# Gate columns in the experts' product, the choice of the expert behind it, and the mixing four groups of steps later

## The reference

```python
p0, p1 = E0[tokens] @ W0 + b0, E1[tokens] @ W1 + b1        # 75 -> 64
alpha = softmax over the two of (p @ Wa + ba);  h = alpha0*p0 + alpha1*p1
x = layernorm(h)
scores = (x @ Q[h].T) @ (x @ K[h].T).T / sqrt(64)          # 8 heads of 32
h = h + sum over heads of softmax(scores) @ x @ VO[h]
x = layernorm(h)
H = gelu(x @ W1 + b1)                                      # 64 -> 256
probs = softmax(H @ Wg + bg);  e = argmax(probs)           # 8 experts
h = h + probs[e] * (H @ Wd[e] + bd[e])
```

## Time and profile before

| | us |
|---|---|
| median of 3 runs | 494.83 |
| lowest, highest | 492.53, 495.33 |
| profiled execution, its own time | 487.88 |
| its span, first to last instruction | 486.0 |
| busy: TensorE, VectorE, ScalarE, GpSimd | 453.8, 330.1, 234.2, 194.1 |

### The profile page before, as it was taken

The page is one execution under the profiler, slowest core; times in us unless marked ns, Lnnn a source line. Parts: engine busy times, 40 slices in busy tenths (PEclk is TensorE's granted clock), DMA queues, the critical chain, the costliest instruction groups (busy, mean ns, idle before and its releaser), DMA issues.

```text
span 486.0 us, 7338 instructions
## 1 busy us (share of the span) xinstructions
PE 453.8 (93%) x2026; PEld 261.1 (54%) x2026; DVE 330.1 (68%) x928; ACT 234.2 (48%) x449; POOL 194.1 (40%) x276
## 2 busy tenths in 40 slices
PE   7699799999899999999999999999999999998985
PEld 6567454556455566456555655556644555444442
DVE  3575657877576776767786768767677858661657
ACT  1203345565734466445735474546643563456330
POOL 4453112422245634365247624463226514361260
PEclk9965689999999999999999999999999999999989
DMA  6072212433232222222232223222222222100000
GB/s 149 23 185 56 53 39 61 113 99 78 50 92 50 61 67 73 68 65 67 77 93 66 51 76 81 56 61 66 71 51 67 65 76 67 34 3 12 0 12 11
DMA packets 24853, 30.97 MB, mean 64 GB/s; under 512 B 9196, under 2 KB 11500, under 8 KB 24812
## 3 DMA queue, kind: packets, MB, share of 16 engines
q1 hardware_dynamic: 22556, 27.05, 22.1%
q0 software_dynamic: 1536, 2.46, 2.3%
q10 hardware_dynamic: 720, 0.98, 0.8%
HBM read 3.99 MB, written 1.05 MB: 10 GB/s over the span
## 4 chain that ended last, share of the span: by engine, by line
PE 71%; DVE 9%; issue 9%; ACT 4%; POOL 2%; SPq 2%; DMA 1%; ACTq 0%; POOLq 0%; DVEq 0%
PE ctx_ps L845 22%; PE st_ps L834 11%; PE s_ps L825 10%; PE sh_ps L925 9%; PE sh_ps L899 5%; PE sh_ps L876 3%; PE sh_ps L914 3%; PE sh_ps L852 3%; DVE neg_max L552 2%; DVE res L696 2%; PE sh_ps L880 2%; PE sh_ps L866 2%; DVE sq L599 1%; SPq L219 1%; ACT prob L410 1%
## 5 line engine op out<-in xcount | busy, mean ns | idle before, releaser
L410 ACT ACTIVATE prob<-st_ps 128x512 f32<-128x512 f32 x256 | 138.6, 594 | 114.3 <-PE st_ps L834 112.8
L552 DVE TENSOR_REDUCE neg_max<-s_ps 128x1 f32<-128x512 f32 x256 | 164.9, 681 | 25.3 <-PE s_ps L825 25.1
L845 PE MATMUL ctx_ps<-prob,xa 128*64 128x512 f32 x512 | 127.1, 619 | 0.0
L825 PE MATMUL s_ps<-kst,qst 96*128 96x512 f32 x256 | 111.0, 480 | 2.5 <-DMA kst<-raw_k 1.3
L834 PE MATMUL st_ps<-qst,kst 98*128 98x512 f32 x256 | 86.5, 415 | 8.4 <-ACT prob L410 8.3
L335 POOL TENSOR_TENSOR zsum<-z 128x256 f32<-128x256 f32 x31 | 23.7, 764 | 104.5 <-DVE z L638 104.5
L845 PEld LDWEIGHTS ctx_ps<-prob,xa 128*64 128x64 f32 x512 | 31.9, 139 | 61.6 <-issue 44.3
L834 PEld LDWEIGHTS st_ps<-qst,kst 98*128 98x128 f32 x256 | 49.5, 195 | 27.2 <-ACT prob L410 14.2
L825 PEld LDWEIGHTS s_ps<-kst,qst 96*128 96x128 f32 x256 | 48.1, 199 | 25.0 <-issue 9.9
L321 POOL TENSOR_TENSOR rstd<-var,half 128x4 f32<-128x4 f32 x16 | 16.5, 1031 | 91.8 <-DVE var L591 91.8
L925 PE MATMUL sh_ps<-wd,hid 128*128 128x512 f32 x96 | 46.8, 610 | 0.0
(11 more groups left out here) (105 smaller groups left out, 522.7 us busy)
## 6 DMA issues: line engine op xcount, KB each, us to landing
qst<-raw_q SPq DMA_DIRECT2D x192, 64.0 KB, 2.0
kst<-raw_k SPq DMA_DIRECT2D x177, 64.0 KB, 2.0
qst<-shift_t SPq DMA_DIRECT2D x64, 4.0 KB
out<-res SPq DMA_DIRECT2D x8, 128.0 KB, 1.8
kst<-raw_k ACTq DMA_DIRECT2D x15, 64.0 KB, 2.1
rows<-emb,idx POOLq DMA_INDIRECT x32, 3.0
wd<-WdT SPq DMA_DIRECT2D x1, 512.0 KB, 4.7
w_raw<-weights SPq DMA_DIRECT2D x2, 192.0 KB, 3.7
```

What stands on the lines that cost most here:

```text
L410: AC.activation(prob[:, t % P_BUFS, :], st_ps[t % ST_BANKS][:, :], ACT.Exp, scale=-1.0).then_inc(p_done, 1)
L552: V.tensor_reduce(neg_max[:, n:n + 1], s_ps[(NT * b + n) % S_BANKS][:, :], AX.X, ALU.min).then_inc(max_done, 1)
L825: PE.matmul(s_ps[k % S_BANKS][:, :], qst[b % 2][0:3 * R, h, c * P:(c + 1) * P], kst[b % 2][0:3 * R, h, :], start=True, stop=True).then_inc ...
L845: last = PE.matmul(ctx_ps[d * C:(d + 1) * C, :], xa[b % 2][:, c, :], prob[:, (2 * m + d) % P_BUFS, :], start=(c == 0), stop=(c == J - 1))
```

## The change

In groups 0 to 5 the gate's eight columns are put in front of the experts' 512, in the weights and in `yb`. The 520 columns don't fit one PSUM bank, so each token tile has two products, `y{j}` with 264 columns and `y{j}b` with 256, in two banks. VectorE adds one bias to both kinds of columns, in two instructions. The gate's own product is left out there, and so is its own bias addition. The rest of the gate is a new name, `choose`, in step 18: maximum and subtraction read the gate's columns of `yb`. `route` moves from step 15 to 19 and the four mixes from 16..19 to 20..23, the store to 24. The experts start a step earlier, 14 to 17. h1 gets a third buffer, since it lives longer. Groups 6 and 7 keep their separate gate and, but for the place within a step, their steps.

```diff
 BEFORE = (
-    ("x_t", -8), ("vo30", 9), ("vo31", 9), ("y1", 16), ("e0_t", -14), ...
+    ("x_t", -8), ("vo30", 9), ("vo31", 9), ("y2", 16), ("y2b", 16), ("e0_t", -14), ...
 BEHIND = (
-    ... ("y2", 17), ("y3", 18), ... ("gate", 14), ("y0", 15))
+    ... ("y3", 17), ("y3b", 17), ... ("gate", 14), ("y0", 14), ("y0b", 14), ("y1", 15), ("y1b", 15))
-    "moments1": 10, "power1": 10, "normal1": 11, "route": 15, "out": 20}
+    "moments1": 10, "power1": 10, "normal1": 11, "choose": 18, "route": 19, "out": 24}
-OTHERS.update({f"mix{j}": 16 + j for j in range(J)})
-OTHERS.update({"ev0": 15, "ev1": 16, "ev2": 17, "ev3": 18})
+OTHERS.update({f"mix{j}": 20 + j for j in range(J)})
+OTHERS.update({f"ev{j}": 14 + j for j in range(J)})
+EARLY = range(B - 2)
-        h1 = [sb(f"h1{n}", [P, J, C]) for n in range(2)]
+        h1 = [sb(f"h1{n}", [P, J, C]) for n in range(3)]
 def gate_logits(dve, b):
+            if b in EARLY:
+                logits = yb[:, :, 0:NE]
+                for j in range(J):
+                    dve.wait_ge(emptied[f"y{j}"], b + 1)
 def y_out(dve, b, j):
-            V.tensor_tensor(yb[:, j, :, :]..., bank(f"y{j}", b)[:, :], bg_bd_s[:, NE:], ALU.add).then_inc(emptied[f"y{j}"], 1)
+            V.tensor_tensor(yb[:, j, 0:YH], bank(f"y{j}", b)[:, 0:YH], bg_bd_s[:, 0:YH], ALU.add).then_inc(emptied[f"y{j}"], 1)
+            dve.wait_ge(filled[f"y{j}b"], b + 1)
+            V.tensor_tensor(yb[:, j, YH:YW], bank(f"y{j}b", b)[:, 0:YW - YH], bg_bd_s[:, YH:YW], ALU.add).then_inc(emptied[f"y{j}b"], 1)
 def experts(pe, b, j):
+            for name, o, width in ((f"y{j}", 0, YH), (f"y{j}b", YH, YW - YH)):
+                claim(pe, name, b)
+                for m in range(M):
+                    last = PE.matmul(bank(name, b)[:, 0:width], hid[b % 2][:, m, j * P:(j + 1) * P], wd[:, m, o:o + width],
+                                     start=(m == 0), stop=(m == M - 1))
+                last.then_inc(filled[name], 1)
```

More of the change, by code:

```diff
@@ L60 @@
 MOVED.update({(name, 1): 2 for name in ("x_t", "q0", "k0")})
[L61 to L64, removed]
+MOVED.update({("y0", B - 2): 3, ("y1", B - 2): 2, ("y2", B - 2): 2, ("route", B - 2): -4, ("out", B - 2): -4, ("out", B - 1): -4})
+MOVED.update({(f"mix{j}", B - 2): -1 for j in range(J)})
+MOVED.update({(f"y{j}", B - 1): 1 for j in range(J)})
+MOVED.update({("route", B - 1): -5})
+MOVED.update({(name, B - 1): -1 for name in ("moments1", "power1", "normal1", "x2_t", "hid0", "hid1", "gate")})
+EARLY = range(B - 2)
+ONLY = {"gate": range(B - 2, B), "choose": EARLY, "y0b": EARLY, "y1b": EARLY, "y2b": EARLY, "y3b": EARLY}
 SPARE = {("y0", B - 2): 0, ("y1", B - 2): 1, ("y2", B - 2): 2, ("y3", B - 2): 3,
@@ L73, in due @@
 def due(s, name):
-    return [b for b in range(B) if GR * b + WHEN[name] + MOVED.get((name, b), 0) == s]
+    return [b for b in ONLY.get(name, range(B)) if GR * b + WHEN[name] + MOVED.get((name, b), 0) == s]
 def claims(s, table):
@@ L337, in accumulate_heads @@
             if p == 0:
[L339 removed]
+                at_least(eng, res_ready, J * (b - 2))
                 before = h_all[:, b, :, :]
             else:
[L342 to L343 removed]
+                before = h1[b % 3][:, :, :]
+            ops.tensor_tensor(h1[b % 3][:, :, :], before, zsum[:, :, :], ALU.add).then_inc(acc_done, 1)
         def mix(pool, b, j):
@@ L527, in _ @@
                     act.preload_act_table_set(EXP_LN)
-                for b in due(s, "gate"):
-                    gate_weights(act, b)
+                for name in ("choose", "gate"):
+                    for b in due(s, name):
+                        gate_weights(act, b)
         def links(dve, name, b, before=0):
@@ L742, in _ @@
                             normalise_heads(dve, b, p, u)
+                for b in due(s, "choose"):
+                    if b == 0:
+                        dve.wait_ge(const_ready, 2)
+                    gate_logits(dve, b)
                 for b in due(s, "k1"):
@@ L794, in _ @@
                     gate_logits(dve, b)
-                for j in (0, 2, 3):
+                for j in (0, 1, 3):
                     for b in due(s, f"ev{j}"):
-                        if b < B - 2:
+                        if b == 0 and j == 0:
+                            dve.wait_ge(late_loaded, LATE_ALL)
+                        if b in EARLY:
                             y_out(dve, b, j)
@@ L921, in expert_part @@
                 claim(pe, name, b)
-                if b >= B - 2:
-                    pe.wait_ge(bias_ready, 3)
-                    PE.matmul(bank(name, b)[:, :], share[:, :], bias[:, :], start=True, stop=False)
-            last = PE.matmul(bank(name, b)[:, :], hid[b % 2][:, m, j * P:(j + 1) * P], wd[:, m, :], start=(m == 0 and b < B - 2), stop=(m == M - 1))
+                pe.wait_ge(bias_ready, 3)
+                PE.matmul(bank(name, b)[:, :], share[:, :], bias[:, :], start=True, stop=False)
+            last = PE.matmul(bank(name, b)[:, :], hid[b % 2][:, m, j * P:(j + 1) * P], wd[:, m, NE:YW], start=False, stop=(m == M - 1))
             if m == M - 1:
@@ L929, in experts @@
         def experts(pe, b, j):
+            if b not in EARLY:
+                for m in range(M):
+                    expert_part(pe, b, j, m)
+                return
             for m in range(M):
-                expert_part(pe, b, j, m)
+                pe.wait_ge(emptied[f"hid{m}"], b + 1)
+            for name, o, width in ((f"y{j}", 0, YH), (f"y{j}b", YH, YW - YH)):
+                claim(pe, name, b)
+                for m in range(M):
+                    last = PE.matmul(bank(name, b)[:, 0:width], hid[b % 2][:, m, j * P:(j + 1) * P], wd[:, m, o:o + width],
+                                     start=(m == 0), stop=(m == M - 1))
+                last.then_inc(filled[name], 1)
         def next_layer_in(pe, b, n):
@@ L958, in _ @@
                         project_out(pe, b, 3, u)
-                for b in due(s, "y1"):
-                    experts(pe, b, 1)
+                for b in due(s, "y2"):
+                    experts(pe, b, 2)
                 for n in range(2):
@@ L1001, in _ @@
                         project_qk(pe, b, 0, which)
-                for b in due(s, "y2"):
-                    experts(pe, b, 2)
                 for b in due(s, "y3"):
@@ L1032, in _ @@
                     else:
+                        if b == 0:
+                            pe.wait_ge(late_loaded, LATE_ALL)
                         experts(pe, b, 0)
+                for b in due(s, "y1"):
+                    experts(pe, b, 1)
 def kernel(x, L0_tok_E0, L0_tok_E1, L0_tok_W0, L0_tok_b0, L0_tok_W1, L0_tok_b1, L0_tok_Wa, L0_tok_ba,
```

58 lines of the change are left out of this document (28 added, 30 removed).

## The result

The changed kernel took 503.43 us (median of 4 runs, 502.25 to 504.87) against 493.68 us (489.46 to 495.33, 4 runs) for the kernel before in the same comparison: a ratio of 1.0212, with a 95% interval of 1.0136 to 1.0289. It is slower. The forecast was 491.0 us, faster; the measured time lies outside its range of 486.4 to 495.0. A repetition gave 507.88 us and a ratio of 1.0367 (1.0259 to 1.0474); both intervals lie above 1. Where the runs of a kernel fall into groups more than 1.5% apart, its ratio is formed from the faster ones, while medians are over all of its runs.

What follows compares the result with a forecast made beforehand. TensorE, busy 453.8 of 486.0 us, was taken as the bound. Groups 0 to 3 gain 0.98 us each (1.60 less a 0.62 wait), groups 4 and 5 nothing; 3.8 off 494.83 gives 491.0 us, range 486.4 to 495.0.

Steps and rivals of the forecast that it cites:

- 9.22 - 7.62 = 1.60 us a group: TensorE, groups 0 to 5: gate, score and old expert products go (9.22), half-width expert products come (7.62).
- (d): Rival on TensorE: weight loads show behind half-width products, net 1.8 us a group slower, 505.6 us; chance 0.02.
- The wait is 277.77 - 277.15 = 0.62 us: Stage 4 transposes: TensorE arrives at 277.15, VectorE's normalisation ends at 277.77; wait 0.62 us, bounds 0 to 1.7.
- -0.98: Each of groups 0 to 3: 1.60 us saved on TensorE less 0.62 us of waiting, so 0.98 us gained.
- the choice leaves stage 7: VectorE, stage 7: moving the choice out frees 1.38 us, cover for the wider eviction, which was priced at nothing.
- as late as before: Groups 4 and 5, stage 3: VectorE's normalisation ends at 383.0 as before, so these groups were taken as 0.
- (a): Rival in stage 3: the VectorE-GpSimd collision is absent or costs little; 7.4 us gained, 487.4 us; chance 0.22.
- (b): Rival in stages 6 and 0: expert second halves wait 0.3 us each for banks, 3.6 us lost, 494.6; chance 0.20.
- (c): Rival in stage 3: VectorE's four sq wait for all of mix 0, late by 1.7 us, 497.6 us; chance 0.06.
- the 0.08 for slower: Total chance given to a measurably slower kernel, beside 0.66 for faster and 0.26 for same.
- The signs I named: Trace marks of being right, among them a stage 4 wait of 0.3 to 1 us and a period of about 51.8.

Runs made afterwards that it cites:

- e7: Changed kernel with GpSimd's mix 0 held until the stage 3 normalisation is written and mix 3 until that of stage 7; 486.6 us, ratio to before 0.9917.
- e8: Changed kernel with the choice of the expert in step 20, behind the normalisation, and mix 3 held until stage 7's normalisation is written; 478.14 us, ratio to before 0.9735.
- e6: Changed kernel with only GpSimd's mix 3 held until the normalisation of stage 7 is written, in four groups; 496.51 us, ratio to before 1.0105.
- e3: Changed kernel with seven 128x128 identity products on TensorE before the x2_t transposes of groups 1 to 6; 494.15 us, ratio to before 1.0046.
- e1: Changed kernel with only GpSimd's mix 0 held until the normalisation of stage 3 is written; runs of 482.87, 483.70, 495.68 and 496.35 us, no ratio formed.

## Why the prediction was wrong

**TensorE's side was right.** The sum 9.22 - 7.62 = 1.60 us a group is what the undisturbed kernels show: 52.78 - 51.22 = 1.56 (e7) and 52.78 - 51.13 = 1.65 (e8). In the chain of the changed kernel the expert pieces are 1.77 and 1.78 behind a shift row, 1.95 behind attention products and 1.82 to 1.89 behind x_t. Rival (d), weight loads that show, is out: no such spacing appears (1.77 for eight products is 0.22 each). By the Trainium skill ("TensorE: Matmul & The Clock Gate", The mechanism), whose list lets a load overlap running matmuls only where its row groups differ, though the same section also names a background weight buffer, the loads for the same row groups would have shown. The 256-column products of the changed kernel do not bear that out here.

**The step that failed first is "The wait is 277.77 - 277.15 = 0.62 us".** The mechanism was the one named, the size was not: it is 1.41. From the start of stage 3's two maxima to the end of the low part the forecast had 277.8 - 269.8 = 8.0; measured 285.54 - 276.93 = 8.61. Of this, the choice took 282.22 - 280.51 = 1.71 where I put 1.38, and the normalisation 285.54 - 282.22 = 3.32 where I put 3.10. The choice is longer because of one instruction, which I had priced as it stood in stage 7, beside an idle GpSimd. VectorE's and GpSimd's timelines of the changed kernel:

```profile
280.51 0.58 DVE L666 TENSOR_SCALAR geq<-gd 128x32 f32<-128x32 f32 x1
...
282.22 2.17 DVE L605 TENSOR_SCALAR sq<-h,mv,rstd 128x64 f32<-128x64 f32 x4
...
298.72 0.96 DVE L633 TENSOR_TENSOR shift_s<-neg_max,shift_s 128x8 fp32r<-128x8 f32 x1
```

```profile
280.34 0.72 POOL L348 TENSOR_TENSOR h<-h_all,zsum 128x256 f32<-128x256 f32 x1
282.44 1.04 POOL L362 TENSOR_TENSOR yc<-yb,coef 128x512 f32<-128x512 f32 x1 [1.38 <-DVE coef L683]
283.56 0.78 POOL L364 TENSOR_TENSOR yc<-yc 128x256 f32<-128x256 f32 x1
```

geq took 0.17 in the earlier trace rows and takes 0.58 here; it ends at 281.09, 0.03 behind the head sum's last addition, which GpSimd began before it. That is 0.41 for 32 elements a partition. The rest of the 0.8 is that the four sq meet two steps of the mix (they end at 284.39, the second step at 284.34), the cast the third (0.59 instead of 0.30), and some 0.2 of start and of TensorE's earlier arrival. With 1.41 instead of 0.62 the term of a full group is -0.2, not -0.98: that alone would have made "no change" of the forecast.

**What was left out of the sum made it slower.** Two terms:

- *Stage 7.* That "the choice leaves stage 7" was booked as cover. But with the mixes four steps later, mix 3 lands there, beside the normalisation of x, which had no mix beside it before: sq 0.97 to 2.49, and 0.88 to 0.90 of waiting in the full periods. I followed mix 0 to its new place and looked for each of the others only whether it came in time, not what it ran beside. e6 shows it by itself.
- *The clock.* I priced every wait at its length. With the wait of 1.4 us at x2_t the granted clock went to 1.2 GHz for 3 to 7 us, which costs 1.6 us and more in a period (e6), more than the wait itself. e3 shows it the other way round. It is the largest of the terms that I missed: of the 3.55 between -0.98 and +2.57 for a full period, 0.79 is the wait that was mis-sized, 0.89 stage 7 and 1.87 the clock.

**Groups 4 and 5** were put at zero ("as late as before"). Their waits are 3.23 and 3.46 against 0.91 and 1.04, and their periods 2.1 and 2.2 longer. The wait follows from the terms above: 0.91 + 1.72 for the product that no longer stands in front is 2.63 at an unchanged finish of VectorE, and 0.33 + 0.22 for the longer choice and normalisation makes 3.18, against 3.23. Those 0.6 are lost outright, and a half clock, at its 1.6, brings it to the 2.2. e6 shows the two apart in group 4: the same wait of 3.23, but full clock, and 52.17 from x2_t to x2_t against 53.69 in the changed kernel and 51.55 before.

**The rivals.** (a), no collision, did not happen in the changed kernel. e7, which keeps the choice in front, makes it happen: 1.56 a full period where (a) had 1.60, and 0.9 and 1.0 in groups 4 and 5 where it had 0.5. That e7's 486.6 is so near (a)'s 487.4 is luck in part, with the clock as low at its end as above. e8 gives 2.4 in each of groups 4 and 5, since there the choice is gone from VectorE's path too. (b), bank and eviction waits, did not come: TensorE's waits for ScalarE are as before within 0.2 us in total (shift row 1.2 over seven in both). (c) was the nearest: VectorE as the bound of stage 3, with a delay that it put at 1.7 and its break-even at 1.6. But the four sq did not wait for the whole mix; they ended behind its second step, and the delay was 1.41. By (c)'s own count the full groups would still have gained 0.2 each. That slower came true is not (c)'s doing but that of the clock and stage 7, which neither it nor the forecast had, so the 0.08 for slower was too small for a reason that stood in no rival.

**The signs I named.** Right: no 8-column products before group 6, the pieces of 1.75 to 1.8, sq near 2 us with the multiplication beside them. Wrong: the wait was to be 0.3 to 1 us, and the period 51.8; it is 55.4.

**What stays open.** What decides whether the clock falls behind a given wait. In e6 the same 1.42 us of waiting is followed by half clock in some groups and not in others; behind 1.66 and 1.90 the clock stayed full in e1, behind 1.90 it was at half in e7. Near the end, the kernel before and e8 both wait for ScalarE's probabilities, 2.34 and 2.31 us, and what follows differs (TensorE's timelines, before and e8):

```profile
443.53 0.98 PE L834 MATMUL st_ps<-qst,kst 98*128 98x512 f32 x2 [2.34 <-ACT prob L410]
444.44 1.94 PE L845 MATMUL ctx_ps<-prob,xa 128*64 128x512 f32 x8
```

```profile
432.17 1.01 PE L853 MATMUL st_ps<-qst,kst 98*128 98x512 f32 x2 [2.31 <-ACT prob L417]
433.11 3.56 PE L864 MATMUL ctx_ps<-prob,xa 128*64 128x512 f32 x8
```

That one difference, 1.6 us, is the +1.7 of e8's last part. Keeping TensorE at work there was not tried. Nor was the exact rule tried by which VectorE is held up beside GpSimd: most rows fit "held until the running instruction ends", the sq of about 309.6 in the changed kernel does not (it outlasts the gather's descriptors and the multiplication behind them), and no run isolates it.

## What to carry to other kernels

When a block moves, ask of every engine that it uses what it will run beside, in each stage it lands in, and not only whether it is in time; a cheap instruction such as a comparison of 32 elements can take the length of another engine's add. A wait of TensorE may cost twice its length, because the clock can fall with it, so a change that trades a saved product for an equal wait can be a loss and not a draw. When a gain is eaten, move the harmful piece and keep the useful one: here the same product was worth 1.65 us a full period once the choice stood behind the normalisation and one mix was held for the other (e8), and 1.56 with both mixes held and the choice in front (e7).

## What the hardware showed

- **VectorE beside GpSimd.** Instructions that read and write SBUF, the memory on the chip, are held up while GpSimd runs a two-input instruction: geq 0.17 to 0.58 beside an add, four sq 0.97 to 2.17 and 2.49 beside a mix, with single ones up to 1.8 us. Those with two tensor inputs can be too: the subtraction for shift_s, 8 elements a partition, takes 0.17 at 287.00 and 0.96 at 298.72 (the last line of VectorE's timeline above), beside the multiplication of 298.62. Maxima from PSUM run at 0.68 us each beside the same mix (mean of all 256: 0.683 in the changed kernel, 0.681 before). GpSimd's own multiplication takes 1.04 or 1.05 with and without VectorE beside it, its second step 0.78 instead of 0.73: the price is nearly all VectorE's. The Trainium skill ("GPSIMD Engine Reference", 8. Key points) speaks of shared interfaces, with contention for VectorE's two-port and two-input forms. The trace agrees for two inputs (0.17 to 0.96, and the low part 0.43 to 0.49, with one 0.63); whether the one-input ones run in a two-port form no row shows.
- **The gather alone hardly does it.** In e8 one of the gather's descriptor instructions runs from 244.88 beside the four sq of 244.34, which take 0.97, and a cast, which takes 0.29. In e6 a cast at 305.28 beside such an instruction takes 0.47.
- **The clock** stays at 2.4 GHz behind the 0.91 us wait of the kernel before at 383.04, and was at 1.2 GHz for 3 to 7 us with all six waits of the changed kernel, which are 1.41 us and longer. e6's groups show both outcomes at 1.41 and 1.42 us, and e1 shows full clock behind 1.66 and 1.90: the length of the wait alone does not decide.
